# Attention layer with layer norms and a ternary feed-forward: where TensorE waits before the value products, and how the flag for lower halves is joined

## The reference, cut to what matters

```python
x = L0_attn_x                                     # 8 x 1024 x 512
x = layernorm(x + attention(x, Wq, bq, Wk, bk, Wv, bv, Wo, bo))
x = layernorm(x + ffn(x, gate_w, up_w, down_w, gate_s, up_s, down_s))

# attention: the softmax runs over the 16 heads of one position, not over positions
q, k, v = (x @ W.T + b).reshape(B, S, H, D) ...   # H = 16, D = 32; q and k are rotated (rope)
qk  = einsum('bshd,bstd->bsht', q, k) / sqrt(D)   # 16 x 16 for each position
out = einsum('bsht,bstd->bshd', softmax(qk), v)
out = swapaxes(out, 1, 2).reshape(B, S, E) @ Wo.T + bo

# ffn: ternary weights, INTER = 1408
out = (silu((x @ gate_w.T) * gate_s) * ((x @ up_w.T) * up_s)) @ down_w.T * down_s
```

## Time and profile before

| | us |
|---|---|
| three runs | 1951.37, 1951.77, 1948.12 |
| median of them | 1951.37 |
| the profiled execution's own time | 1946.58 |
| its span, first to last instruction | 1944.8 |
| its mean granted TensorE clock | 0.984 |
| its attention phase, up to the barrier | about 936.5 |

### The profile page before, as it was taken

The page is one execution under the profiler, slowest core; times in us unless marked ns, Lnnn a source line. Parts: engine busy times, 40 slices in busy tenths (PEclk is TensorE's granted clock), DMA queues, the critical chain, the costliest instruction groups (busy, mean ns, idle before and its releaser), DMA issues.

```text
span 1944.8 us, 41042 instructions
## 1 busy us (share of the span) xinstructions
PE 1835.3 (94%) x15488; PEld 1474.9 (76%) x15488; DVE 1188.0 (61%) x1734; ACT 714.1 (37%) x1138; POOL 740.4 (38%) x571
## 2 busy tenths in 40 slices
PE   6899999999999999996599999999999999999997
PEld 5677777777777777775488888888888888888885
DVE  6688888888888888886234444344443444434443
ACT  4444555445544545443222222222222222222221
POOL 5676777777877777673010111001110011101111
PEclk9999999999999999998799999999999999999998
DMA  6346555665566645665601112011110111101011
GB/s 196 102 122 166 140 138 138 163 165 131 135 148 165 145 137 137 160 181 143 223 13 64 57 42 65 33 65 38 59 65 32 65 38 59 65 32 65 33 32 43
DMA packets 257790, 194.47 MB, mean 100 GB/s; under 512 B 143056, under 2 KB 182608, under 8 KB 257744
## 3 DMA queue, kind: packets, MB, share of 16 engines
q1 hardware_dynamic: 257744, 193.84, 36.2%
HBM read 109.13 MB, written 84.67 MB: 100 GB/s over the span
## 4 chain that ended last, share of the span: by engine, by line
PE 41%; issue 9%; POOL 1%; DVE 0%; DMA 0%; ACT 0%; POOLq 0%; DVEq 0%; SPq 0%; ACTq 0%
PE ps_g L829 7%; PE ps_g L826 7%; PE ps_u L826 7%; PE ps_u L829 7%; PE acc L846 7%; PE acc L843 7%; POOL z L909 1%; DMA dscale<-down_s 0%; DVE xT_lo L978 0%; DVE z L958 0%; POOL rs L911 0%; POOLq L698 0%; DVE hid L926 0%; ACT act_g L876 0%; DVE z L940 0%
## 5 line engine op out<-in xcount | busy, mean ns | idle before, releaser
L926 DVE SCALAR_TENSOR_TENSOR hid<-ps_u,gu_scale,act_g 128x512 f32<-128x512 f32 x176 | 132.1, 751 | 450.7 <-ACT act_g L876 450.7
L909 POOL TENSOR_TENSOR z<-z,wide 128x512 f32<-128x512 f32 x64 | 80.7, 1293 | 731.0 <-DVE z L940 731.0
L876 ACT ACTIVATE act_g<-ps_g,gu_scale 128x512 f32<-128x512 f32 x176 | 121.4, 690 | 574.3 <-PE ps_u L829 574.3
L324 PE MATMUL ps_x<-w_hi,xc_hi 128*128 128x512 f32 x768 | 309.1, 402 | 17.3 <-POOL xc_lo L477 7.9
L325 PE MATMUL ps_x<-w_lo,xc_hi 128*128 128x512 f32 x768 | 305.3, 398 | 0.0
L326 PE MATMUL ps_x<-w_hi,xc_lo 128*128 128x512 f32 x768 | 305.0, 397 | 0.0
L497 POOL TENSOR_TENSOR qk_cos<-qk_in,rot 128x512 f32<-128x512 f32 x128 | 204.1, 1595 | 165.7 <-DVE qk_in L572 141.3
L843 PE MATMUL acc<-wf_rest,hid_hi 128*128 128x512 f32 x640 | 252.6, 395 | 1.2 <-DVE hid_lo L932 1.2
L829 PE MATMUL ps_g<-xT_lo,wf_rest 128*128 128x512 f32 x640 | 253.2, 396 | 0.0
L846 PE MATMUL acc<-wf_rest,hid_lo 128*128 128x512 f32 x640 | 252.8, 395 | 0.0
L826 PE MATMUL ps_u<-xT_hi,wf_rest 128*128 128x512 f32 x640 | 252.6, 395 | 0.0
(11 more groups left out here) (85 smaller groups left out, 2955.6 us busy)
## 6 DMA issues: line engine op xcount, KB each, us to landing
xc<-x_cols SPq DMA_DIRECT2D x32, 512.0 KB, 4.4
v_rows<-v_in SPq DMA_DIRECT2D x32, 512.0 KB, 3.2
v<-v_rows SPq DMA_DIRECT2D x32, 512.0 KB, 5.5
res<-x_rows SPq DMA_DIRECT2D x64, 256.0 KB, 2.9
x_rows<-x_out SPq DMA_DIRECT2D x32, 512.0 KB, 3.3
x_cols<-x_turn SPq DMA_DIRECT2D x128, 128.0 KB, 2.4
wide<-x_rows SPq DMA_DIRECT2D x16, 1024.0 KB, 5.5
out<-z SPq DMA_DIRECT2D x64, 256.0 KB, 3.1
```

The lines of the kernel that those rows point to most:

```text
L324: pe.matmul(out, hi[:, k], w_hi[:, w, k], start=(k == 0), stop=False)
L926: dve.scalar_tensor_tensor(out=hid[:, :], in0=slot(u, j)[1][:, :], scalar=gu_scale[:, 1, j:j + 1], in1=act_g[:, :], op0=ALU.mult, op1=ALU. ...
```

## The change

Two edits. First: in the loop, the four waits of `inputs_of_av` move from in front of the second output projection to in front of its last product, eleven products later. `project` has a new argument for that. Second: the maximum over the partitions is replaced by a product with a column of ones on TensorE, which adds the 128 values up (they are absolute values, so the sum is over zero when one of them is). It is done in step UNITS + 1 = 33, after the value products: DVE reduces `lo_top`, TensorE multiplies into one element of `ps_x[0]`, DVE makes `inexact` of it, for partition 0 alone. GpSimd fills `ones` at the start.

```diff
+        ones = sb("ones", [P, 1])
...
-            def project(out, hi, lo, w, sem_done, first_use):
+            def project(out, hi, lo, w, sem_done, first_use, next_av=None):
...
                     pe.matmul(out, hi[:, k], w_lo[:, w, k], start=False, stop=False)
+                    if k == KE - 1 and next_av is not None:
+                        inputs_of_av(next_av)
                     last = pe.matmul(out, lo[:, k], w_hi[:, w, k], start=False, stop=(k == KE - 1))
...
-                        if t == 1 and not isinstance(s, int):
-                            inputs_of_av(s - 2)
                         project(ps_x[2 + t][:, :], aT_hi[:, t], aT_lo[:, t], 3, o_done,
-                                isinstance(m, int) and m == 0 and t == 0)
+                                isinstance(m, int) and m == 0 and t == 0,
+                                next_av=s - 2 if t == 1 and not isinstance(s, int) else None)
...
+                if isinstance(s, int) and s == UNITS + 1:
+                    pe.wait_ge(lo_reduced, 1)
+                    pe.matmul(ps_x[0][0:1, 0:1], lo_top1[:, :], ones[:, :], start=True, stop=True).then_inc(lo_joined, 1)
...
-            pool.wait_ge(power_set, 2)
+            pool.memset(ones[:, :], 1.0).then_inc(power_set, 1)
+            pool.wait_ge(power_set, 3)
...
-                if isinstance(s, int) and s == UNITS + 2:
-                    pool.wait_ge(lo_reduced, 1)
-                    pool.partition_all_reduce(lo_top1[:, 1:2], lo_top1[:, 0:1], P, bass.bass_isa.ReduceOp.max)\
-                        .then_inc(lo_joined, 1)
...
-                if isinstance(s, int) and s == UNITS + 2:
+                if isinstance(s, int) and s == UNITS + 1:
                     dve.wait_ge(lo_seen, SLABS)
-                    dve.tensor_reduce(lo_top1[:, 0:1], lo_top[:, :], AX.X, ALU.max).then_inc(lo_reduced, 1)
+                    dve.tensor_reduce(lo_top1[:, :], lo_top[:, :], AX.X, ALU.max).then_inc(lo_reduced, 1)
+                    dve.wait_ge(lo_joined, 1)
+                    dve.tensor_scalar(shared.inexact[0:1, :], ps_x[0][0:1, 0:1], 0.0, None, ALU.is_gt)\
+                       .then_inc(flag_set, 1)
...
-            dve.wait_ge(lo_joined, 1)
-            dve.tensor_scalar(shared.inexact[:, :], lo_top1[:, 1:2], 0.0, None, ALU.is_gt).then_inc(flag_set, 1)
             dve.wait_ge(flag_set, 1)
```

More of the change, by code:

```diff
@@ L199, in attention_phase @@
         lo_top = sb("lo_top", [P, SLABS])
-        lo_top1 = sb("lo_top1", [P, 2])
+        lo_top1 = sb("lo_top1", [P, 1])
+        ones = sb("ones", [P, 1])
         ps_x = [ctx.enter_context(nc.psum_tensor(f"ps_x{b}", [P, E], F32)) for b in range(4)]
```

## The result

The changed kernel takes 1914.7 us (median of four runs, 1913.05 to 1916.59) against 1950.3 for the kernel before (four runs, 1948.12 to 1951.77): a ratio of 0.9819, 95% interval 0.9802 to 0.9836, 35.6 us less. Forecast were 1917.1 us, 34.3 less. The profiled execution took 1914.57 us, its span 1912.8, at a mean granted clock of 0.982.

What follows compares the result with a forecast made beforehand. TensorE, busy for 94% of the span, was taken to set the pace. 26.5 us from the moved waits plus 7.8 at the border make 34.3, so 1951.37 - 34.3 = 1917.1 us, range 1909 to 1930.

Steps and rivals of the forecast that it cites:

- The price of a stop: TensorE's wait for `pX` before the second output projection: 0.94 us lost plus 0.08 behind it, 1.02 us a step.
- The room at the new place: Before the twelfth product of the second output projection: `pX` is complete 2.06 us before it is needed.
- Who is late next: Loop work behind the moved waits: with value products 1.02 us earlier, no other late input reaches TensorE.
- Number of steps: Loop steps that gain: 26 of 27, step 5 left out for its scores' 1.13 us stop; 26.5 us gained.
- The reduction over partitions: At the border of the phases: without GpSimd's reduction `var_eps` of step 34 starts earlier, 7.8 us gained.
- The join on TensorE: Step 33: reduction, product with ones and comparison, some 0.8 us, fit into VectorE's 1.10 us wait; no cost.
- TensorE's restart: Behind the border wait: again at 1.2 GHz for six or seven products; no change taken, 1.3 us either way.
- A: Rival: the waits' own work shows at the new place in the loop; gain 24.5 us, 1926.9 us; chance 0.11.
- B: Rival: VectorE's chain bounds the loop, so only the border's gain is left; 1943.6 us; chance 0.05.
- C: Rival: GpSimd's 7.29 us at the border are not the reduction and stay; 1924.9 us; chance 0.05.
- D: Rival: the loop's streams of small products run short of instructions; slower, 1971.1 us; chance 0.03.
- E: Rival: neither part of the change acts; no change, 1951.4 us; chance 0.01.

Runs made afterwards that it cites:

- spread_first: Changed kernel, but the wait for `pX` stands before the projection's first product, the other three before the twelfth; 1935.3 us against 1951.0 for the kernel before.
- flag_only: Changed kernel with the four waits put back in front of the projection, only the product with ones kept; 1944.8 us against 1951.0 for the kernel before.
- gpsimd_ready: Changed kernel, but GpSimd's reduction in step 34 replaces the product with ones, VectorE reducing `lo_top` in step 33; 1919.2 us against 1951.5 for the kernel before.
- no_join: Changed kernel without reduction of `lo_top`, product with ones and comparison, flag set to zero by memset; 1915.9 us against 1950.5 for the kernel before.

## Why the prediction was right, and where it was off

Forecast were 34.3 us, measured 35.6, and 33.5 when the same kernel was measured again. The mechanism of both parts is shown below; that the number is so close rests in part on small terms that cancelled.

*What bounds the kernel:* right. TensorE set the pace; taking 1.01 us a step out of its own stream came out of the time in full.

*The price of a stop, 1.02 us of idle time and refill:* right; the step fell by 1.01. Its two halves were told apart as the prediction had them: of the 0.40 for the waits' own work three of the four waits are 0.31 (`spread_first`), and the last 0.09 are what the one wait for `pX` takes more in the loop (0.14) than with constants (0.05). The rest is `pX` itself, 0.49 us later than the product could start, the handover of 0.05 and the refill of 0.08: 1.02 together.

*The room at the new place, 2.06 us:* borne out, 2.08 in the trace. At the twelfth product nothing is left of the wait; at the fourth, where the same reckoning gave 0.24 us and a refill, 0.14 and 0.08 were left.

*Who is late next:* nobody, right. One detail was off: I let VectorE's `y` take 0.1 us from the wait for the scores; that wait is 1.10 as before, and `y` starts 0.11 us behind the first value product in both kernels.

*Number of steps:* too few by one. I left step 5 out because its scores stop for instructions, and coming 1.02 us earlier might only lengthen that stop, to some 2.1 us. It did not: the stop is 1.13 us before and 1.00 in `flag_only`, and 0.73 to 1.50 in the nine profiles with all four waits at the twelfth product. From the value products of step 4 to those of step 6 are 60.7 and 60.3 us with the waits in their old place and 58.0 to 59.8 in these nine. With 27 steps the term is 27.3, and the sum 35.1 in place of 34.3. The medians, with intervals of 3 us to either side, can't tell 26 steps from 27.

*The reduction over partitions, 7.8 us:* right by the traces. `var_eps` comes 7.8 us sooner behind `mean_var`, and the piece from step 33 on is 7.8 us shorter. That these two agree so well is luck: a load that landed 0.4 us sooner and products at the lower clock that took 0.4 us longer cancelled, and with the flag alone the piece is 6.9 us shorter (1030.3). The flag alone, by its medians, gives 6.2, with an interval of 4.3 to 9.8 us (0.9978 and 0.9950 of 1951.0). I took the reduction for 7.7 us of GpSimd's time; it is 12.9, of which the kernel before hid the first part. That changed nothing here, and spoilt the expectation for `gpsimd_ready`.

*The join on TensorE, nothing:* right. My estimate of 0.8 us is 0.58 in the trace, within the 1.10 that VectorE waits there, and `no_join` is not faster.

*TensorE's restart:* the wait is 16.7 us where 17.1 was expected, since the load of `dscale` took 0.4 us less. I took no change for the products at 1.2 GHz behind it; it was one more, 0.4 us with the rest of the restart, and two more in the second profile, within my bound of 1.3. I did not see that TensorE stands at a branch for 5.8 us of the wait; it lies beside the load and the split, so it didn't touch the sum.

*Profile and median:* I noted that the profiled execution lay 4.8 us under the median and forecast from the median. That choice was right. Against the profile alone the span gained 32.0 us, not 35.6, and the difference lies in the start of the program.

*Rivals:* each is ruled out by a measurement. A (waits exposed): 0.32 us from the twelfth product to the value products. B (another chain takes over): no new wait in the loop. C (the border gives nothing): 0.08 us from `mean_var` to `var_eps`. D (starved streams): no stop inside the small products in a loop pass after the first. E (no effect): two gains that add up.

## What to carry to other kernels

A wait belongs as late in its engine's stream as the data allow, with long work queued in front of it: even conditions that have long been met cost time when the queue is empty (0.31 us a pass for three here), and nothing behind eleven long products. Work out the moment when each place would be due and compare it with the moment when the data are complete; here that reckoning held for the fourth and the twelfth product to 0.1 us. Compare executions piece by piece, cut at an instruction that recurs, before trusting a difference of spans, and when a wait in series is removed, look in the engine's own queue for what runs beside it: at this border two edits that each gained nothing gave 3 to 4 us together. Look too at what the moved wait held back behind it: here a table load of 1.28 us that had been hidden came onto ScalarE's path.

## What the runs showed of the hardware

- A branch of TensorE to code that stood behind the other version took 5.29 to 5.89 us in eleven profiles, and 0.07 us in the two where the wanted version stood right behind it; in these two the jump over the other version came at the end of the phase instead, with 3.5 and 3.7 us. The Trainium skill, "Runtime: NRT & Kernel Launch", section "Instruction fetch mechanics", says that a taken branch outside the fetched window waits for a fetch of its target; these rows agree, with a price for it.
- GpSimd's reduction over 128 partitions of one column took 12.9 us of the engine, though the trace shows an instruction of 0.38 us: 5.4 us stand before it and 7.1 behind it as "issue", each behind two MODIFY_POOL_CONFIG on its sequencer. TensorE's product with a column of ones did the same job in 0.58 us, VectorE's part included.
- TensorE, standing with an empty queue behind ScalarE, starts 0.05 us after `pX` when its four waits are on constants, 0.14 us with only the wait for `pX` on a register's value there (beside that for the bank), and 0.45 us with the other three there too.
- The same start of the program, with the same instructions, took 178 to 183 us over thirteen profiles. In the two compared above, the granted clock between 60 and 90 us was 0.94 in the shorter and 0.83 in the longer; over all thirteen the clock does not order the times.
- ScalarE's table load in front of a silu took 1.28 us. It ran unseen when only the data's wait stood in front of the silu, and after that wait when a second one stood there too.
